# Row maxima of attention scores from high parts alone, two heads side by side on the array's rows

## The reference

```python
q = _l2norm(q) * q_scale
k = _l2norm(k) * k_scale
sim = jnp.einsum('bhid,bhjd->bhij', q, k) * SCALE
sim = sim + slopes * bias
sim = jnp.where(causal[None, None], -neg, sim)
attn = jax.nn.softmax(sim, axis=-1)
out = jnp.einsum('bhij,bhjd->bhid', attn, v)
```

## Time and profile before

| what | value |
|---|---|
| time, median of 3 runs | 3890.81 us (3886.72 to 3895.19) |
| time of the profiled execution | 3888.84 us |
| its span, first to last instruction | 3886.7 us |
| TensorE busy | 3410.9 us, 88% of the span |
| VectorE busy | 3246.1 us, 84% |
| ScalarE busy | 2830.7 us, 73% |
| GpSimd busy | 2006.9 us, 52% |
| mean granted clock of TensorE | 0.933 of full speed |

### The profile page before, as it was taken

The page is one execution under the profiler, slowest core; times in us unless marked ns, Lnnn a source line. Parts: engine busy times, 40 slices in busy tenths (PEclk is TensorE's granted clock), DMA queues, the critical chain, the costliest instruction groups (busy, mean ns, idle before and its releaser), DMA issues.

```text
span 3886.7 us, 97861 instructions
## 1 busy us (share of the span) xinstructions
PE 3410.9 (88%) x35857; PEld 2291.0 (59%) x35857; DVE 3246.1 (84%) x8403; ACT 2830.7 (73%) x5453; POOL 2006.9 (52%) x2052
## 2 busy tenths in 40 slices
PE   1689989898998989889988998989989899898998
PEld 0356666565665656656665666656656566665665
DVE  6788888788887888888887888888888788887886
ACT  2477777677777778777787777777777677777776
POOL 2564455645556445554447445474454744556443
PEclk7789999999999999999999999989999899999999
DMA  3000000000010000100001001010000000000000
GB/s 129 21 15 2 21 21 31 20 2 23 18 37 15 2 23 26 34 10 2 29 23 39 2 4 34 23 31 2 15 26 29 23 2 23 18 34 12 2 2 23
DMA packets 41335, 82.39 MB, mean 21 GB/s; under 512 B 5792, under 2 KB 5792, under 8 KB 40352
## 3 DMA queue, kind: packets, MB, share of 16 engines
q1 hardware_dynamic: 36864, 67.13, 5.5%
q10 hardware_dynamic: 4000, 9.02, 0.6%
HBM read 59.36 MB, written 16.78 MB: 20 GB/s over the span
## 4 chain that ended last, share of the span: by engine, by line
PE 41%; DVE 24%; POOL 15%; issue 12%; ACT 7%; DMA 0%; ACTq 0%; POOLq 0%; DVEq 0%
DVE PS L780 5%; PE PS L969 5%; PE PS L970 5%; PE PS L971 5%; POOL RN L641 5%; PE PS L955 4%; DVE PL L850 4%; DVE Q2T L877 4%; PE PS L990 3%; PE PS L991 3%; PE PS L1032 2%; POOL QKB L634 2%; POOL STR L645 2%; DVE QKB L914 2%; ACT TOK L477 2%
## 5 line engine op out<-in xcount | busy, mean ns | idle before, releaser
L442 ACT ACTIVATE PR<-PS,BT,SC 128x512 f32<-128x512 f32 (+3 forms) x1536 | 1024.0, 667 | 360.0 <-PE PS L993 318.2
L780 DVE CUSTOM_DVE_ANT_0 PS<-PS,STR 128x512 f32<-128x512 f32 (+3 forms) x1536 | 834.4, 566 | 107.7 <-PE PS L955 97.7
L447 ACT ACTIVATE PH<-PR 128x512 f16<-128x512 f32 (+3 forms) x1536 | 804.0, 523 | 48.7
L850 DVE TENSOR_TENSOR PL<-PR,PH 128x512 f16<-128x512 f32 (+3 forms) x1152 | 692.5, 601 | 2.4 <-ACT PH L447 2.1
L641 POOL TENSOR_TENSOR RN<-SS,HALF 128x8 f32<-128x8 f32 x256 | 422.8, 1652 | 522.8 <-DVE SS L863 520.4
L969 PE MATMUL PS<-WH,XT 128*128 128x384 f16 x2048 | 671.3, 328 | 18.6 <-DVE QKB L801 18.6
L1022 PE MATMUL PS<-AR,PH 128*128 128x66 f16 x4608 | 612.7, 199 | 74.2 <-ACT PH L447 40.0
L970 PE MATMUL PS<-WL,XT 128*128 128x384 f16 x2048 | 669.7, 327 | 0.0
L971 PE MATMUL PS<-WH,XT 128*128 128x384 f16 x2048 | 669.6, 327 | 0.0
L593 POOL TENSOR_TENSOR PL<-PR,PH 128x512 f16<-128x512 f32 x384 | 449.1, 1169 | 423.2 <-ACT PH L447 416.5
L955 PE MATMUL PS<-AR 128*128 128x512 f16 (+3 forms) x1536 | 542.6, 353 | 137.6 <-DVE MX L780 91.4
(11 more groups left out here) (178 smaller groups left out, 7364.8 us busy)
## 6 DMA issues: line engine op xcount, KB each, us to landing
XW<-in_L_attn_x SPq DMA_DIRECT2D x128, 256.0 KB, 2.6
ACC<-in_L_attn_x SPq DMA_DIRECT2D x64, 256.0 KB, 2.6
out<-ACC SPq DMA_DIRECT2D x64, 256.0 KB, 2.0
AR<-in_L_attn_Wkv ACTq DMA_DIRECT2D x1, 4096.0 KB, 20.4
AR<-in_L_attn_Wq ACTq DMA_DIRECT2D x1, 2048.0 KB, 11.3
ACC<-in_L_attn_Wout ACTq DMA_DIRECT2D x1, 2048.0 KB, 25.1
LG<-in_L_ffn_ln_g ACTq DMA_DIRECT2D x1, 256.0 KB, 5.6
LB<-in_L_ffn_ln_b ACTq DMA_DIRECT2D x1, 256.0 KB, 5.8
```

The source lines that it names most:

```text
L442: e.activation(PR[:, n % 3, 0:wide], PS[:, n % 2, 0:wide], ACT.Exp, bias=BT[:, 2 * (u % NP) + h, kt - 4 * qc + 4:kt - 4 * qc + 5], scale=S ...
L447: e.activation(PH[:, n % 4, 0:wide], PR[:, n % 3, 0:wide], ACT.Copy).then_inc(s_ph, 1)
L780: e.tensor_tensor_reduce(out=r[:, 0:n], in0=r[:, 0:n], in1=ST[:, h, o:o + n], scale=1.0, scalar=LOW, op0=ALU.add, op1=ALU.max, accum_out=M ...
L850: e.tensor_tensor(PL[:, n % 3, 0:wide], PR[:, n % 3, 0:wide], PH[:, n % 4, 0:wide], ALU.subtract).then_inc(s_pl, 1)
```

## The change

The maxima are now taken of high parts alone: 64 rows of q against 64 rows of k. So that both heads of a pair can use the array at once, the tile of k of the second head is laid out the other way round (low part in the first 64 columns of TOK, high part in the next), which puts its high parts into rows 64 to 127 of KQ. A piece is now one query tile and one run of keys for both heads: two matmuls, on rows 0 to 63 and on rows 64 to 127, into two banks of the ring. There are 12 such pairs in a unit, in slots 13, 15, 17, 19, and 21 to 28, by turns ahead of the score matmuls (13, 17, 21, 23, 25, 27) and behind them. The low parts of k and the copies into K2 are written head by head, by two instructions in place of one.

```diff
-PIECES = [(h, qt, c) for g in range(4) for qt in (2 * g, 2 * g + 1) for h in range(2) for c in range(1 + qt // 4)]
+PIECES = [(qt, c) for qt in range(NT) for c in range(1 + qt // 4)]
...
         for u, i in due(s, W_PIECE[0]):
-            take("s", u, i)
+            take("s", u, 2 * i)
+            take("s", u, 2 * i + 1)
...
+        KHI = bass.AP(tok.tensor, tok.offset + 512, [tok.ap[0], (320, 2), (P, 2), (1, 64)])
...
-                    e.activation(TOK[:, 2:4, :, 0:64], QKB[:, i % 2, 2:4, :, :], ACT.Copy, scale=KA).then_inc(s_hi, 1)
+                    e.activation(KHI, QKB[:, i % 2, 2:4, :, :], ACT.Copy, scale=KA).then_inc(s_hi, 1)
...
-                w.wait_ge(s_s, 24 * u + i + 1)
+                w.wait_ge(s_s, 24 * u + 2 * i + 2)
...
-                r = rb("s", u, i)
-                e.tensor_tensor_reduce(out=r[:, 0:n], in0=r[:, 0:n], in1=ST[:, h, o:o + n], scale=1.0, scalar=LOW,
-                                       op0=ALU.add, op1=ALU.max, accum_out=MX[:, qt // 4, qt % 4, h, c:c + 1]).then_inc(s_mx, 1)
+                for h in range(2):
+                    r = rb("s", u, 2 * i + h)
+                    e.tensor_tensor_reduce(out=r[:, 0:n], in0=r[:, 0:n], in1=ST[:, h, o:o + n], scale=1.0, scalar=LOW,
+                                           op0=ALU.add, op1=ALU.max,
+                                           accum_out=MX[:, qt // 4, qt % 4, h, c:c + 1]).then_inc(s_mx, 1)
...
-                    e.tensor_copy(K2[0:64, u % 2, :, 256 * g:256 * g + 256],
-                                  KQ[0:64, u % 2, 2:4, 256 * g:256 * g + 256]).then_inc(s_k2, 1)
+                    for h in range(2):
+                        e.tensor_copy(K2[0:64, u % 2, h, 256 * g:256 * g + 256],
+                                      KQ[64 * h:64 * h + 64, u % 2, 2 + h, 256 * g:256 * g + 256]).then_inc(s_k2, 1)
...
-                    e.scalar_tensor_tensor(
-                        out=TOK[:, 2:4, :, 64:128].rearrange("p j a c -> p (j a) c"),
-                        in0=QKB[:, i % 2, 2:4, :, :].rearrange("p j a c -> p (j a) c"), scalar=KA,
-                        in1=TOK[:, 2:4, :, 0:64].rearrange("p j a c -> p (j a) c"), op0=ALU.mult, op1=ALU.subtract).then_inc(s_lo, 1)
+                    for h in range(2):
+                        hi, lo = slice(64 * h, 64 * h + 64), slice(64 - 64 * h, 128 - 64 * h)
+                        e.scalar_tensor_tensor(out=TOK[:, 2 + h, :, lo], in0=QKB[:, i % 2, 2 + h, :, :], scalar=KA,
+                                               in1=TOK[:, 2 + h, :, hi], op0=ALU.mult, op1=ALU.subtract).then_inc(s_lo, 1)
...
-                h, qt, c = PIECES[i]
+                qt, c = PIECES[i]
                 n = min(512, P * (qt + 1) - 512 * c)
-                bank_free(w, "s", u, i)
+                bank_free(w, "s", u, 2 * i)
+                bank_free(w, "s", u, 2 * i + 1)
                 w.wait_ge(s_kq, 4 * u + qt // 2 + 1)
-                e.matmul(rb("s", u, i)[:, 0:n], KQ[:, u % 2, h, P * qt:P * qt + P], KQ[:, u % 2, 2 + h, 512 * c:512 * c + n],
-                         start=True, stop=True).then_inc(s_s, 1)
+                for h in range(2):
+                    hs = slice(64 * h, 64 * h + 64)
+                    e.matmul(rb("s", u, 2 * i + h)[:, 0:n], KQ[hs, u % 2, h, P * qt:P * qt + P],
+                             KQ[hs, u % 2, 2 + h, 512 * c:512 * c + n], start=True, stop=True).then_inc(s_s, 1)
```

More of the change, by code:

```diff
@@ L35 @@
 SLOPES = [2.0 ** (-0.5 * (i + 1)) for i in range(H)]
-PIECES = [(h, qt, c) for g in range(4) for qt in (2 * g, 2 * g + 1) for h in range(2) for c in range(1 + qt // 4)]
-PIECE_G = [[i for i, z in enumerate(PIECES) if z[1] // 2 == g] for g in range(4)]
+PIECES = [(qt, c) for qt in range(NT) for c in range(1 + qt // 4)]
+PIECE_G = [[i for i, z in enumerate(PIECES) if z[0] // 2 == g] for g in range(4)]
 def piece_slots(odd):
@@ L220, in fused_block @@
         NKT = TOK[0:64, 0, 0, :]
+        tok = TOK[:, :, :, :]
+        KHI = bass.AP(tok.tensor, tok.offset + 512, [tok.ap[0], (320, 2), (P, 2), (1, 64)])
         IOI = PL[:, 0, :].bitcast(I32)
@@ L428, in _ @@
                     if g > 1:
-                        w.wait_ge(s_lo, 2 * (g - 1))
+                        w.wait_ge(s_lo, 3 * (g - 1))
                     if u > 1:
@@ L988, in _ @@
                     w.wait_ge(s_q2, 2 * u + qc + 1)
-                    w.wait_ge(s_k2, 4 * u + kt // 2 + 1)
+                    w.wait_ge(s_k2, 8 * u + 2 * (kt // 2) + 2)
                     e.matmul(bank, KQ[:, u % 2, 2 + h, ks], KQ[:, u % 2, h, q0:q0 + wide], start=True, stop=False)
@@ L1051, in _ @@
                     w.wait_ge(s_hi, 2 * i + 2)
-                    w.wait_ge(s_lo, 2 * i + 2)
+                    w.wait_ge(s_lo, 3 * i + 3)
                     for j in range(4):
@@ L1086, in _ @@
                     w.wait_ge(s_c, 2 * u + qc + 1)
-                    w.wait_ge(s_lo, 2 * (4 * u + 2 * qc + 1) + 2)
+                    w.wait_ge(s_lo, 3 * (4 * u + 2 * qc + 1) + 3)
                     for h in range(2):
```

## The result

The changed kernel takes **4019.39 us** (median; 4017.57 to 4020.45), the kernel before 3889.18 us in the same comparison: a ratio of 1.0332, 95% interval 1.0314 to 1.035, or 130 us slower. The forecast was 54 us slower. The direction was right, the size was not, and the time lies 4 us above the range.

What follows compares the result with a forecast made beforehand. Bound by TensorE in slots 0 to 4 and 13, by VectorE in 17 to 22. Terms 0.02 + 0.21 + 0.34 + 0.13 (low parts) + 0.14 (K2 copies) = 0.84 us, times 64 units 54 us: 3943 us, range 3888 to 4015.

Steps and rivals of the forecast that it cites:

- Pieces on TensorE: Pairs' halved columns against 0.18 us of switches and a 0.03 step: slots 1 to 4 +0.02 us a unit, slot 13 +0.21.
- Slot 13's term: On TensorE in slot 13, one piece of 0.05 us becomes 0.05 + 0.21: +0.21 us a unit.
- Rival B: The two heads' matmuls run one after the other, keeping their columns and paying the switches: 4001 us, chance 0.14.
- rival A: Switch nearly free, heads overlap: -0.24 us a unit, 3873 us; said to decide from under 0.12 us a pair; chance 0.08.
- The hand-over: In slot 23 the pair waits for its bank behind VectorE's maxima: 0.58 us later, 0.24 absorbed, +0.34 us a unit.
- The other waits that change: VectorE's wait for both matmuls of a pair and three engines' waits on s_lo, given no added time.
- The others I cost at nothing: VectorE's split instructions in slots 9, 11, 15 and 23, covered by other engines' work: 0; uncovered, 0.68 us a unit.
- C: Costs hide: half the switch price, a quarter of hand-over and split costs; about -0.07 us a unit, 3884 us, chance 0.08.
- D: All VectorE costs counted as covered come out: 44 us more, 3987 us, inside the forecast's bounds, no chance of its own.
- The signs of being wrong: Ordinary step into a pair, second matmul 0.22 us behind the first, or slots 17 to 22 changing over 0.5 us.

Runs made afterwards that it cites:

- all_but_narrow: Kernel before with the pairs' order and banks, split low parts and split K2 copies, but 128-row matmuls and the old layout: 4014.89 us, ratio 1.0323.
- last_ahead: Changed kernel with a unit's last pair placed ahead of slot 4's score matmuls instead of behind them: 3989.77 us, ratio 1.0238.
- lo_split: Kernel before with the low parts of k written in two instructions of 128 elements in place of one of 256: 3938.68 us, ratio 1.0115.
- q2t_later: Kernel before with VectorE's remainder of q one slot later and ScalarE's eviction of k waiting for the low parts alone: 3842.38 us, ratio 0.9875.

## Why the prediction was half right

The parts run by themselves are 46 (order and banks), 45 (low parts), 51 (K2) and 4 (narrow matmuls in place). The first three give 142 us, together 126 (all_but_narrow). The 16 us between may be shared by them, but the uncertainty of the sum is some 13.

- **Pieces on TensorE, +0.02 and +0.21: the price was right.** The switch costs 0.20 us a pair (forecast 0.18 + 0.03), the heads overlap wholly, and slots 1 to 4 change by +0.05 through the narrow matmuls. Slot 13's term falls into slot 12 by my boundaries, since the pair stands ahead of slot 13's scores; hence the window of slot 13 is unchanged. Slot 12 grew by 0.23, but by 0.14 with 128-row matmuls too, so that term is borne out by the pair's price and not by the slot. Reading the price from a neighbour with another tile, worked. Rival B falls with the 0.004 us, rival A with the 0.20. A's limit was miscounted: its own terms, six switches against -0.24, cancel at 0.04 us a pair and not at 0.12; the measured price is above both. Slot 0 got no term, though the earlier trace rows has TensorE busy for all of it: its pair of 256 columns saves 0.11 and pays 0.20, and it waits 0.16 for its bank.
- **The hand-over, +0.34: did not come out.** Pairs wait longer for their banks (TensorE at L967 on L787 111.1 us, at L955 on L780 91.4 before), but with the order alone slots 14 to 4 grow by 0.03, and the wait stands in slot 22, not in slot 23. I had followed one slot to its end and not asked whether the slots before it got shorter; slot 21 did.
- **"The other waits that change": the step that failed first.** It named the wait for both matmuls of a pair and that on s_lo, and missed that the unit's last pair delays the shift. It is 0.58 us in slot 5, 37 us in all, shown by last_ahead. The prediction's stretches ended with slot 4 and began again with slot 13.
- **VectorE, "The others I cost at nothing": the step that failed most.** The cover hardly held. The low parts were +0.73 a unit, not 0.26, and the K2 copies 0.8 by the medians (51 us by 64; 1.06 in the profiled execution), not 0.14. For the low parts of slot 17 the text named no cover at all. Two errors stand behind it. The sizes came from undisturbed instructions, while the groups by form had 735 ns on average, 0.41 in the row I took; and a copy that changes rows was priced like one that doesn't. And cover by another engine's work did not hold: in slots 14 to 4 lo_split alone adds 0.58.
- **Rivals C and D.** C falls. D, that covered costs come out, was what happened, at more than its price. I gave it no chance of its own, and the range took in no case of D with a new wait beside it: 54 + 44 + 37 would have been 135 us. That this is close to 130 would have been luck in part, since the 54 hold 22 us of a hand-over that did not come out, and VectorE's instructions cost more than D's price.
- **The signs of being wrong.** None of the three came: the step into a pair is 0.26 and not 0.16, the second matmul is 0.004 behind and not 0.22, and slots 17 to 22 are within 0.25 us (13.74 against 13.97 in the units shown, 15.23 against 15.07 as means). They watched terms that had a price, and the failure lay in those that had none.

What stays open: how the 45 us of the low parts divide between GpSimd's exclusion and the longer list, the clock's part in the 49 us of q2t_later, and what makes the clock fall in more units.

## What to carry to other kernels

Price an instruction by its group's mean and spread over the whole trace, not by one clean row: if the mean is nearly twice the clean one, something else sets its length, and splitting it can pay that twice. When a step is regrouped, follow the last element of the group to its consumer, even outside the stretches that the change touches. A layout that helps one engine moves work to whoever must undo it; here two 64-row tiles came out about even on TensorE, and the split low parts, the crossing copies and the pairs' order (45, 51 and 46 us by themselves) made them a loss.

## What the runs showed of the hardware

- Going from 128-row to 64-row matmuls and back costs about 0.10 us each way (0.096 and 0.107). The Trainium skill, TensorEngine Tiling (Array Packing), Key Properties, says that a change of mode drains the engine; the runs give the price. So, by an estimate from 0.20 us for both ways and 0.216 for 512 columns, a pair gains only above some 480 columns.
- Matmuls in two 64-row tiles start 0.003 to 0.006 us apart. The Trainium skill, TensorE: Matmul & The Clock Gate, Measured speedup vs the span model, gives about 4 ns for each tile; the trace agrees.
- VectorE's low parts and remainder, which have two SBUF inputs, stand still until the running GpSimd instruction ends, and end 0.148 us (128 elements) or 0.28 us (256) behind it. q2t_later, which parts one of them from GpSimd's squares and shortens a wait of ScalarE's, is 49 us faster than the kernel before.
- A VectorE copy from rows 64 to 127 into rows 0 to 63 doesn't overlap its neighbours: 0.25 us for each of two, against 0.14 where both read rows 0 to 63.
